# A two-layer graph kernel: the first gathers paced, dense slices moved, layer-norm scales deferred, all products halved by VectorE

## The reference

```python
h = jnp.maximum(_layernorm(x, axis=-1), 0.0)
x = x + _L0_gnn_ref(h, src, dst, edge_attr_3, edge_attr_10, edge_weight, W1, W2)
h = jnp.maximum(_layernorm(x, axis=-1), 0.0)
x = x + _L1_gnn_ref(h, edge_index, Wq, Wk, Wv, Wout)
```

## Time and profile before

| | us |
|---|---|
| median of three runs | 1520.99 (1516.53 to 1529.5) |
| the profiled execution | 1531.05 |
| its span | 1528.7 |
| VectorE busy | 926.1 |
| POOL busy | 824.9 |
| PE busy | 784.7 |
| ScalarE busy | 674.3 |
| mean granted TensorE clock | 0.701 of full |

### The profile page before, as it was taken

The page is one execution under the profiler, slowest core; times in us unless marked ns, Lnnn a source line. Parts: engine busy times, 40 slices in busy tenths (PEclk is TensorE's granted clock), DMA queues, the critical chain, the costliest instruction groups (busy, mean ns, idle before and its releaser), DMA issues.

```text
span 1528.7 us, 15502 instructions
## 1 busy us (share of the span) xinstructions
PE 784.7 (51%) x4772; PEld 626.0 (41%) x4772; DVE 926.1 (61%) x1689; ACT 674.3 (44%) x1671; POOL 824.9 (54%) x795
## 2 busy tenths in 40 slices
PE   0066676666766676767764133435343369970000
PEld 0055555555555555555652022212221169960000
DVE  4266676666666665667735877557587889970000
ACT  0056565656565656566634336546451122210000
POOL 6545555555555455552008886637470038877775
PEclk9987978797879787978875565656555555555555
DMA  3111110112111102110027249858673100000000
GB/s 59 36 44 30 34 34 14 30 34 58 19 30 35 33 14 55 34 32 10 23 80 165 33 46 86 54 96 75 75 52 57 30 3 10 9 10 10 10 11 9
DMA packets 40519, 60.36 MB, mean 39 GB/s; under 512 B 17347, under 2 KB 30935, under 8 KB 40182
## 3 DMA queue, kind: packets, MB, share of 16 engines
q0 software_dynamic: 25184, 12.32, 15.6%
q1 hardware_dynamic: 12074, 46.84, 9.3%
q10 hardware_dynamic: 3180, 0.21, 0.2%
HBM read 40.33 MB, written 19.36 MB: 39 GB/s over the span
## 4 chain that ended last, share of the span: by engine, by line
DVE 21%; PE 17%; issue 16%; ACT 13%; POOL 13%; DMA 6%; DVEq 6%; another core or an unknown queue 6%; SPq 0%; POOLq 0%; ACTq 0%
POOL out_dram L623 13%; PE sums L986 10%; DVE h1d_or_products L1317 4%; DMA src_everywhere<-src_by_columns 3%; DVE h1d_or_products L1308 3%; ACT agg_or_stacks L708 2%; ACT agg_or_stacks L717 2%; ACT L738 2%; PE turnB L962 2%; ACT stack_turned L717 2%; DVEq L1307 2%; PE tens L976 2%; DVE dstat L1336 2%; ACT below L816 2%
## 5 line engine op out<-in xcount | busy, mean ns | idle before, releaser
L590 POOL DMA_INDIRECT x_rows<-in_x,src_index x196 | 185.1, 944 | 258.7 <-PE tens L980 218.2
L986 PE MATMUL sums<-h1d_or_products,ident 128*128 128x192 f32 (+1 forms) x1344 | 285.8, 369 | 39.5 <-issue 29.3
L623 POOL DMA_INDIRECT out_dram<-agg_or_stacks,scatter_index x196 | 210.4, 1074 | 161.5 <-DVE agg_or_stacks L1683 99.5
L614 POOL DMA_INDIRECT agg_or_stacks<-run_sums,sum_row_index x196 | 231.4, 1180 | 115.8 <-DVE features_or_scores L1591 57.0
L986 PEld LDWEIGHTS sums<-h1d_or_products,ident 128*128 128x128 f32 x1344 | 249.7, 235 | 61.7 <-issue 44.6
L590 POOL DMA_INDIRECT x_rows<-in_x,dst_index x196 | 193.9, 989 | 64.9 <-issue 64.9
L1317 DVE TENSOR_TENSOR h1d_or_products<-tens,hid 128x768 f32<-128x768 f32 x168 | 156.5, 950 | 104.3 <-PE tens L980 104.3
L1055 PE MATMUL small<-one_column,steps 128*128 128x1 f16 x196 | 38.1, 195 | 167.8 <-DVE steps L1466 70.3
L1055 PEld LDWEIGHTS small<-one_column,steps 128*128 128x128 f16 x196 | 24.7, 126 | 196.5 <-ACT below L816 73.0
L726 ACT ACTIVATE h1d_or_products<-tens,hid 128x48 f32<-128x48 f32 x448 | 87.7, 330 | 0.0
L717 ACT COPY agg_or_stacks<-turnA 96x896 bf16<-96x896 bf16 x42 | 37.9, 902 | 91.8 <-PE turnA L962 46.5
(11 more groups left out here) (273 smaller groups left out, 2162.5 us busy)
## 6 DMA issues: line engine op xcount, KB each, us to landing
src_everywhere<-src_by_columns SPq DMA_DIRECT2D x14, 896.0 KB
xin<-in_x SPq DMA_DIRECT2D x27, 449.5 KB
out_dram<-xin SPq DMA_DIRECT2D x27, 449.5 KB
x_rows<-in_x,src_index POOLq DMA_INDIRECT x196
x_rows<-in_x,dst_index POOLq DMA_INDIRECT x196
run<-run_sums SPq DMA_DIRECT2D x1, 3136.0 KB
agg_or_stacks<-run_sums,sum_row_index POOLq DMA_INDIRECT x196
out_dram<-agg_or_stacks,scatter_index POOLq DMA_INDIRECT x196
```

The source lines that it names most:

```text
L590: nc.gpsimd.indirect_dma_start(xs[:, t, side, :], None, x, bass.IndirectOffsetOnAxis(ap=idx[:, t:t + 1], axis=0)).then_inc(s_gath[g % LEAD ...
L614: nc.gpsimd.indirect_dma_start(aggr[:, t, :], None, rs, bass.IndirectOffsetOnAxis(ap=ridx[:, t:t + 1], axis=0)).then_inc(s_rsg[g % LEAD2], 16)
L623: nc.gpsimd.indirect_dma_start(out, bass.IndirectOffsetOnAxis(ap=sidx[:, t:t + 1], axis=0), aggr[:, t, :], None, bounds_check=N - 1, oob_i ...
L986: mm = nc.tensor.matmul(sums[:, a * OUTS:b * OUTS].rearrange("p (c o) -> p c o", o=OG), ident[:], prod[:, 2 * a:2 * b, j, :], start=(j == ...
```

## The change

Four parts, with no change of the computed function:

1. **First gathers.** Tiles 0 to 9 are gathered without a wait. Tiles 10 to 22 wait for marks of the first group, one each (`paced`); beyond that the rule is as before, with AHEAD = 23.
2. **Dense slices.** 21 slices in phase one (groups with g % 4 != 3; sums, centring, square, variance in group g, root there, scale and add in g + 1), 7 in phase two (g % 4 == 1, all in one group). SP's queue in phase two goes by groups.
3. **Deferred scales.** Phase two works with relu(centred rows), unscaled, made by ScalarE beside the square. The sums of squares are kept; after group 28 one root and one reciprocal over 392 columns give the scales of the dst rows and of the sources, their product multiplies the scores, the sources' scale multiplies the weights, and the dst rows' scale is put on h where `ysum` is made.
4. **Halving.** `halve_rest(g-1)` on VectorE, between product 0 and 1 of group g, adds the upper eight terms of tiles 3 to 6 of group g-1 to the lower eight (128x1536 results), and `sum_rest` has 8 terms instead of 16.

```diff
     NP = NG // 2
+    SLICE1 = {g: d for d, g in enumerate(g for g in range(NG) if g % 4 != 3)}
+    SLICE2 = {g: len(SLICE1) + d for d, g in enumerate(g for g in range(NG) if g % 4 == 1)}
+    assert len(SLICE1) + len(SLICE2) == ND
+
     MARKS = (0, 10, 18, NG - 2, NG)
...
     LEAD1 = 4
-    AHEAD = 24
+    AHEAD = 23
     LEAD2 = 8
...
             spread_src(0)
-            for k in range(NP):
-                store(k)
-                load(k + 2)
-                if 2 * k in MARKS[1:]:
-                    store_runs(MARKS.index(2 * k) - 1)
+            for g, d in SLICE1.items():
+                store(d)
+                load(d + 2)
+                if g in MARKS[1:]:
+                    store_runs(MARKS.index(g) - 1)
             store_runs(len(MARKS) - 2)
...
-            for k in range(NP):
-                if k + C1 < NCHUNK - 1:
-                    sp.wait_ge(s_S, k + (C1 + 1))
-                    spread_src(k + (C1 + 1))
-                store(k + NP)
-                if k + NP + 2 < ND:
-                    load(k + NP + 2)
+            for g in range(NG):
+                if g % 2 == 0 and g // 2 + C1 < NCHUNK - 1:
+                    sp.wait_ge(s_S, g // 2 + (C1 + 1))
+                    spread_src(g // 2 + (C1 + 1))
+                if g in SLICE2:
+                    store(SLICE2[g])
+                    if SLICE2[g] + 2 < ND:
+                        load(SLICE2[g] + 2)
...
             nc.gpsimd.tensor_copy(identb[:], ident[:]).then_inc(s_id, 1)
+            def paced(t):
+
+                if t == 10:
+                    pool.wait_ge(s_gsb, 1)
+                elif t == 11:
+                    pool.wait_ge(s_w2p, 1)
+                elif t == 12:
+                    pool.wait_ge(s_cen, 1)
+                elif t == 13:
+                    pool.wait_ge(s_h, 1)
+                elif t == 14:
+                    pool.wait_ge(s_hi, 1)
+                elif t == 15:
+                    pool.wait_ge(s_lo, 1)
+                elif 15 < t < 20:
+                    pool.wait_ge(s_turned, t - 15)
+                elif 20 <= t < AHEAD:
+                    pool.wait_ge(s_tens, min(t - 19, 2))
+                elif t >= AHEAD:
+                    pool.wait_ge(s_tens, t - AHEAD + 1)
+
             pool.wait_ge(s_src, 16 * 3)
...
                     pool.wait_ge(s_cen, g - LEAD1 + 1)
-                if t >= AHEAD:
-                    pool.wait_ge(s_tens, t - AHEAD + 1)
+                paced(t)
                 for side, idx in enumerate((idx_s, idx_d)):
...
                 act.wait_ge(s_dc, half + 1)
-                nc.scalar.activation(cols(run, half, T // 2), cols(h1d, half, T // 2), ACT.Square).then_inc(s_dq, 1)
-
-            def dst_deviation(half):
-                act.wait_ge(s_dv, half + 1)
-                nc.scalar.activation(cols(stat_d[:, 2, :], half, T // 2), cols(stat_d[:, 1, :], half, T // 2),
-                                     ACT.Sqrt, bias=eps[:, 0:1], scale=1.0 / FEAT).then_inc(s_dd, 1)
+                nc.scalar.activation(cols(run, half, T // 2), cols(h1d, half, T // 2), ACT.Square)
+                nc.scalar.activation(cols(h1d, half, T // 2), cols(h1d, half, T // 2), ACT.Relu).then_inc(s_dq, 1)
             for half in range(2):
                 dst_square(half)
-                dst_deviation(half)
             def src_square(g, b):
                 act.wait_ge(s_bc, g + 1)
-                nc.scalar.activation(q1s[:, b], c1s[:, b], ACT.Square).then_inc(s_bq, 1)
-
-            def src_deviation(g, b):
-                act.wait_ge(s_bv, g + 1)
-                nc.scalar.activation(stat_b[:, b, 2, :], stat_b[:, b, 1, :], ACT.Sqrt, bias=eps[:, 0:1],
-                                     scale=1.0 / FEAT).then_inc(s_bd, 1)
+                if past(g, 1):
+                    act.wait_ge(s_bv, g - 1)
+                nc.scalar.activation(q1s[:, b], c1s[:, b], ACT.Square)
+                nc.scalar.activation(cols(aggr, g), c1s[:, b], ACT.Relu).then_inc(s_bq, 1)
             def stage_rows(g):
...
             group2(NP - 1, 1, False)
+            act.wait_ge(s_bv, NG)
+            nc.scalar.activation(stat_d[:, 2:4, :], stat_d[:, 2:4, :], ACT.Sqrt, bias=eps[:, 0:1],
+                                 scale=1.0 / FEAT).then_inc(s_bd, 1)
             act.wait_ge(s_sm, 1)
...
                 if half == 0:
-                    pe.wait_ge(s_tfree, (g + 1) * NDV)
-                    pe.wait_ge(s_tact, g + 1)
-                mm = sum_tiles(TACT, GA, half * HID // 2, (half + 1) * HID // 2, HID)
+                    pe.wait_ge(s_half2, g + 1)
+                mm = sum_tiles(TACT, GA, half * HID // 4, (half + 1) * HID // 4, HID // 2)
                 if half == 1:
...
                 v.tensor_tensor(stack[:, :, SLOTS - 1, :], rest, stack[:, :, 1, :], ALU.subtract).then_inc(s_lo, 1)
+            def halve_rest(g):
+                v.drain()
+                dve.wait_ge(s_tact, g + 1)
+                v.tensor_tensor(prod[:, 2 * TACT:, 0:HID // 2, :], prod[:, 2 * TACT:, 0:HID // 2, :],
+                                prod[:, 2 * TACT:, HID // 2:, :], ALU.add).then_inc(s_half2, 1)
+
             def halve(g):
...
                 multiply(g, b, 0)
+                if past(g, 0):
+                    halve_rest(g - 1)
                 multiply(g, b, 1)
...
                     row_sums(k + 1, b)
-                if b == 1:
-                    dense_scale(k)
-                    dense_add(k)
+                if g - 1 in SLICE1:
+                    dense_scale(SLICE1[g - 1])
+                    dense_add(SLICE1[g - 1])
                 else:
...
                     centre(g + 2)
-                if b == 0:
-                    dense_sums(k)
+                if g in SLICE1:
+                    dense_sums(SLICE1[g])
                 if past(g, 0):
...
                     messages(g - 1, 1 - b)
-                if b == 0:
+                if g in SLICE1:
                     if not past(g, 0):
                         v.drain()
-                    dense_centre(k)
+                    dense_centre(SLICE1[g])
                 multiply(g, b, 2)
...
                     variance(g + 2)
-                if b == 0:
-                    dense_variance(k)
+                if g in SLICE1:
+                    dense_variance(SLICE1[g])
                 multiply(g, b, 6)
...
             group(NP - 1, 1)
+            halve_rest(NG - 1)
             outputs(NG - 1, 1)
...
                 dve.wait_ge(s_dq, half + 1)
-                v.tensor_reduce(cols(stat_d[:, 1, :], half, H), cols(run, half, H), AX, ALU.add).then_inc(s_dv, 1)
-
-            def dst_h(half):
-                dve.wait_ge(s_dd, half + 1)
-                v.reciprocal(cols(stat_d[:, 3, :], half, H), cols(stat_d[:, 2, :], half, H))
-                v.drain()
-                v.scalar_tensor_tensor(cols(h1d, half, H), cols(h1d, half, H), 0.0,
-                                       spread(cols(stat_d[:, 3, :], half, H), 2, [P, H, FEAT]), ALU.max, ALU.mult
-                                       ).then_inc(s_h1d, 1)
-
-            dst_h(0)
+                v.tensor_reduce(cols(stat_d[:, 2, :], half, H), cols(run, half, H), AX, ALU.add)
             def source_rows(k, b):
...
                     search_steps(k + C1)
-                if b == 0:
-                    dense_sums(k + NP)
+                if g in SLICE2:
+                    dense_sums(SLICE2[g])
                     v.drain()
-                    dense_centre(k + NP)
+                    dense_centre(SLICE2[g])
                 dve.wait_ge(s_bq, g + 1)
-                v.tensor_reduce(stat_b[:, b, 1, :], q1s[:, b], AX, ALU.add).then_inc(s_bv, 1)
-                if b == 0:
-                    dense_variance(k + NP)
+                v.tensor_reduce(cols(stat_d[:, 3, :], g), q1s[:, b], AX, ALU.add).then_inc(s_bv, 1)
+                if g in SLICE2:
+                    dense_variance(SLICE2[g])
                 if fits(g + 1):
                     source_rows(k + b, 1 - b)
-                dve.wait_ge(s_bd, g + 1)
-                v.reciprocal(stat_b[:, b, 3, :], stat_b[:, b, 2, :])
-                v.drain()
-                v.scalar_tensor_tensor(cols(aggr, g), c1s[:, b], 0.0, spread(stat_b[:, b, 3, :], 2, [P, GA, FEAT]),
-                                       ALU.max, ALU.mult)
-                if b == 0:
-                    dense_scale(k + NP)
+                if g in SLICE2:
+                    dense_scale(SLICE2[g])
                 v.drain()
...
                                 spread(cols(aggr, g), 2, [P, GA, HEADS, FEAT]), ALU.mult).then_inc(s_qfree, 1)
-                if b == 0:
-                    dense_add(k + NP)
+                if g in SLICE2:
+                    dense_add(SLICE2[g])
                 v.drain()
...
             source_rows(0, 0)
-            dst_h(1)
             group2(0, 0, True)
...
             group2(NP - 1, 1, False)
+
+
+            rows_scale, src_scale, both_scale = stat_d[:, 2, :], stat_d[:, 3, :], stat_d[:, 1, :]
```

(12 more changed lines are left out.)

27 lines of the change are left out of this document (12 added, 15 removed).

## The result

The changed kernel takes 1457.12 us (median of 4 runs, 1453.94 to 1463.03), the kernel before on the same chip 1523.74 (4 runs): 0.957 times as long, 95% interval 0.9512 to 0.9627. 1430 was forecast, between 1395 and 1475. The profiled run took 1460.19 (span 1457.0). The two spans differ by 71.7 us.

| stretch, us | before | after | difference | forecast |
|---|---|---|---|---|
| to product five of group 0 | 100.1 | 87.1 | -13.0 | -5 |
| from there to that of group 27 (27 periods) | 677.7 | 660.9 | -16.8 | -5 |
| to the first search step of phase two | 114.0 | 106.4 | -7.6 | -11 |
| nine pairs with search | 231.3 | 220.6 | -10.7 | -48 |
| last five pairs | 87.2 | 52.5 | -34.7 | -30 |

What follows compares the result with a forecast made beforehand. No engine was full, so stages were read by their waits, largest in phase two. Terms -5 -5 -2 -9 -78 +5 +2 = -92 took the profiled 1531.05 us to 1439, about 1430 as a median, range 1395 to 1475.

Steps and rivals of the forecast that it cites:

- the prediction's own signs of being wrong: Groups above 27 us, product five's wait over 5, s_h after 70, or phase two's nine pairs above 215 us.
- the sign of being right: In phase two, nine pairs at 20 us with VectorE waiting for src_everywhere or gathered rows.
- Nine pairs: Phase two's pairs with search: bound by transfers and GpSimd, 185 us against 232.7, so -48, range -20 to -70.
- That rival (1462): Phase two, store ahead of the spread: SyncE still waits for stores, nine pairs some 217 us, total 1462; chance 0.15.
- Last five pairs: Phase two's pairs without search: 17.1 us each to 8.2 plus two slices, say 55 in all: -30, range -20 to -35.
- Prologue: Before phase one: marks end stalls beside 48 unbroken gathers, s_h 12 us earlier; net -5, range -20 to +8.
- 7 back: Prologue: tiles 13 to 19 released one by one, so group 2's rows land late and 7 us are lost.
- Phase one: 28 groups: halving and seven more slices add some 92 us to VectorE's waits; -0.15 a group, -5, bounds -25 and +20.
- the slower rival (1560): VectorE becomes phase one's bound: all 92 us exposed, phase two returning 47; +38, total 1560, chance 0.04.
- Shared port: VectorE's two-input operations can hold up GpSimd's descriptors: 28 halvings would cost GpSimd 50 us, inside its 165 of waiting.
- The forecast's +2: Phase three: what comes before the first scatter and a slower cadence of the first groups give +2, range 0 to 5.
- Dst rows and middle: Dst rows lose two reciprocals and two products: -9 (-10 to -4); middle gains reciprocal, root and products: +5 (3 to 8).

Runs made afterwards that it cites:

- Kernel 9: The changed kernel with 128 zero rows, one per partition, in place of the one shared zero row; 1472.34 us, 0.9684 of the kernel before.
- kernel 6: The changed kernel issuing only 8 of a pair's 14 gathers from chunk five on, the other rows filled with zeros; 1439.16 us in a single run.
- kernel 8: The changed kernel with GpSimd waiting, before a group's third gather in phase two, until the group before's gathers have landed; 1456.51 us, 0.9504 of the kernel before.
- kernel 10: kernel 8 with room for 10 groups ahead instead of 8 (LEAD2 = 10); 1460.9 us, 0.9662 of the kernel before.
- kernel 11: The kernel before with only the wait for landed gathers of kernel 8 added; 1495.13 us, 0.9839 of the kernel before.
- kernel 3: The changed kernel with 14 dense slices in each of phases one and two; 1489.58 us, 0.9712 of the kernel before.
- kernel 1: The changed kernel with first gathers released as in the kernel before: AHEAD = 24, no marks; 1485.95 us, 0.9692 of the kernel before.
- kernel 4: The changed kernel with phase two's layer-norm scales taken at once, as in the kernel before; 1478.94 us, 0.964 of the kernel before.
- kernel 5: The changed kernel itself again, as base for the runs beside it; 1468.48 us, 0.958 of the kernel before.
- kernel 7: The changed kernel with a chunk's gathers from chunk 5 on in three lots (5, 5, 4), let go after comparisons; 1454.98 us, 0.9485 of the kernel before.
- kernel 2: The changed kernel without halve_rest, TensorE summing 16 terms of tiles 3 to 6 again; 1510.83 us, 0.9836 of the kernel before.
- kernel 12: kernel 8 and kernel 9 together, the wait only in groups 10 to 21; 1401.88 us, 0.992 of the kernel before on its chip.

## Why the prediction was right or wrong

The measured 1457 lies inside 1395 to 1475, and in part that is luck. The nine pairs missed their term by 37 us; the prologue, phase one and the last five pairs came 8, 12 and 5 us better than forecast and made good 25 of them. One of the prediction's own signs of being wrong, nine pairs above 215 us, came true (220.6), and VectorE did not wait for src_everywhere or gathered rows there, as the sign of being right had it, but 77.5 us for comparisons.

**Nine pairs, -48 forecast, -10.7 measured: the step that failed** is "Phase two therefore becomes bound by transfers and GpSimd, not by VectorE". It was worked out from the gathers' share of the DMA engines, 1.20 us of all engines each. Kernel 9 takes that share away and the pair keeps its length; kernels 6 and 8 shorten the run of gathers, and behind the first pair most pairs fall to 16 to 21 us. What bounded it in place of transfers is ScalarE's comparisons, held for signals of TensorE until the run of 14 gathers is over or nearly so. Before, the burst began some 10 us after the search step, when a buffer came free, and the last comparisons came 5 to 8 us into it, unheld; only in its first two pairs, beside and just behind a run of 74 gathers, were some held, by 2.5 to 4.0 us. The faster VectorE frees the buffers sooner, so the burst starts with the index at the search step itself, and the comparisons run into its late part. The change made its own wait. That the unbroken run does it is shown by kernels 6, 8, 10 and 11 on two chips, and kernel 9 rules out the DMA engines as the cause. Whether the delay sits in TensorE or in the passing of its signal is open: in the pair shown the trace has the products of all 14 tiles, the last ended at 906.88, but their ends are modelled. The first pair, which grew by 11.9 us, had no term of its own in the forecast.

The Trainium skill, "DMA: Bandwidth & Descriptors", section Queues, rings and completion order, has each DMA engine take turns between its queues, a packet at a time; the prediction inferred that a store among gathers keeps the next spread waiting. That rival (1462) gave the time nearest to the result, and yet for the wrong reason. Its 10 us for a store were also too many: the earlier trace rows have 1857 packets for 56 gathers, two for each engine and gather, so eight of them are four gathers, some 5 us. SyncE's waits for stores sank to 26.5 us in three, and in the nine pairs src_everywhere was waited for no more.

**Last five pairs**, -30: -34.7, right in mechanism and size, as kernel 3 shows (31 us for its share of the slices).

**Prologue**, -5: -13.0. The mark was under-priced: s_h moved by 31 us, not 12, since nearly all the idle time before it goes (39 us of VectorE's from 24 us to s_h before, 7 after). Of that, 18 are lost again, 11.69 in one wait before product five, while the gathers let go by the mark run from 58.7 to 84.7 without a pause; the "7 back" for late rows stood for it.

**Phase one**, -5: -16.8 (its -0.15 a group is -4 over 28 groups). Before the mix the working held: 14.1, 14.1, 13.0 and 10.5 were forecast for the cycle of four, and 14.06, 14.05, 13.0 and 12.2 or 10.8 came. What was missed lies behind the mix. The wait of 18.0 us for ScalarE was counted; `gate`'s wait for ScalarE, 15.8 us in 19 times in the same window, was not on the list, and it is gone as well: a later mix finds ScalarE done. That is 0.8 us a group. With it the terms make 26 us over 27 periods, more than the 16.8, so this account of phase one does not close. Product five's wait stayed (72.5), as forecast, and slid past as a whole, so the slower rival (1560) fell: with 92 us of new work on VectorE, the periods shrank. That rival's 47 us back from phase two also have no source in the working, which had 78 there; with 78 it is some 1530. How much the periods shrank is less sure than the table says: nearly the same phase one (kernel 1 lacks the marks) took 666.8 to 675.5 us in the profiles of kernels 1 and 4 to 10, and the kernel before 677.7 and 677.4 (kernel 11), so 16.8 is the best of nine, and on the chip where both were profiled it is 7 to 9 us, near the forecast.

**Shared port.** The 392 gathers of x_rows hold GpSimd for 379.0 us before and 425.5 after (224.9 for dst, as above, and 200.6 for src), 46.5 more. The Trainium skill, "SBUF — State Buffer", section on SBUF as two separate sides, has a VectorE operation with two SBUF inputs lock a port against a GpSimd operation that reads SBUF; that such a gather counts as one is the prediction's inference. It gave 50 us here, and the sum agrees. Yet it isn't 28 halvings at 1.76 us each: without them (kernel 2) the gathers take 391.7 us, and with them but without marks (kernel 1) 401.4. In the changed kernel 24 gathers that overlap a halving are longer by 29.2 us together than their usual 0.945 us each, in kernel 1 as many by 18.9; the rest is beside other products. How much is lost depends on where the gathers fall between VectorE's operations. It costs no time in phase one, since GpSimd's wait sinks by more. In phase three it has a price: a scatter's mean rises from 1074 to 1102 ns, 196 times 28 ns are 5.5 us, and the scatters' stretch grew by 5.7; in kernel 4, without the 28 deferred products, the mean is 1073 ns and the stretch 282.3. The forecast's +2 left that out. Kernel 2 doesn't fit: 1088 ns, but a stretch of 295.0, which stays unexplained.

**Dst rows and middle.** The stretch to the first search step of phase two lost 7.6 instead of 11: the dst part gave the -9 (9.4), and the end of phase one rose by 1.9 where -2 was forecast. The middle's +5 came as +5.3; its new reciprocal on VectorE's timeline:

```profile
1127.49 2.59 DVE L1626 RECIPROCAL stat_d<-stat_d 128x392 f32<-128x392 f32 x1
```

It is 2.59 us for 392 columns, where at most 3.0 was allowed.

## What to carry to other kernels

Before an engine is made faster, look at what its work releases, and when: here VectorE's shorter work freed buffers sooner and so let a burst of gathers go just ahead of the comparisons that the next step needed, and three quarters of a stage's expected gain stayed there. A share of DMA time tells that engines are held, not that the kernel waits for them; spread the addresses and see whether anything moves. Where long runs of GpSimd's gathers lie beside work of other engines that must signal each other, a wait for landed gathers inside the run is worth trying: it gave 24 us (kernel 11) and 38 us (kernel 8) in the nine pairs, though kernel 8 lost 28 of them again where the rows came late. The best versions measured, kernels 7 and 8, stand at 0.9485 [0.9449, 0.9522] and 0.9504 [0.9464, 0.9545], where the changed kernel on the same chip has 0.958 [0.9547, 0.9613].

## What the hardware showed that was not expected

- Beside an unbroken run of GpSimd gathers, ScalarE's wait for TensorE's signals grows: the last comparisons came 20.7 us after the search step with 14 gathers in a run, 13.2 to 15.4 with eight. In the changed kernel's runs of 14 the first hold began 11 to 14 us into the run, in a run of seven (kernel 8) a hold of 2.4 us began after 6.2; beside 70 gathers it reached 10.32 us. This is on three chips; on a fourth a run of 28 held nothing (kernel 12), and there the kernel before took 1408.28 us instead of 1518 to 1536. How much of the change's gain is left on such a chip is open: the changed kernel didn't run there.
- Gathers of which many rows read one address held 45.5% of the DMA engines; with 128 such addresses, 5.4% (kernel 9), and the kernel was no faster for it.
- The same halvings on VectorE raised the mean of the dst gathers from 989 to 1147 ns with the marks and only to 997 without them (kernel 1).
